# First-layer mixture of experts taken per batch half, its biases as bf16 rows, and the next attention begun on the first half

## The reference, cut to what matters

```python
# L0_ffn: x has L = 2 "positions" (the batches), so softmax over two keys
y1 = ln(x + mha(x), ln1_g, ln1_b)                 # 4 heads of 32
gates = softmax(y1 @ wg)                          # 8 experts, top one
keep = (rank of the token within its expert) < 128    # tokens counted in order
h = disp @ w1 + b1                                # no activation between
y = h @ w2 + b2
y2 = ln(y1 + where(keep, gate * y, 0), ln2_g, ln2_b)
x = ln(x + y2)
# L1_attn: 16 heads of 64 over 512 keys of the same batch
q, k, v = x @ w_q, x @ w_k, x @ w_v
x = ln(2 * x + softmax(q k^T / 8) v @ w_o)
```

## Time and profile before

| what | us |
|---|---|
| median of the runs | 761.89 |
| the profiled execution | 762.34 |
| its span, first to last instruction | 760.5 |
| mean granted clock of TensorE | 0.942 of full speed |
| PE busy / DVE / ACT / POOL | 686.6 / 455.1 / 278.2 / 238.8 |

### The profile page before, as it was taken

How to read it: one execution, slowest core, us unless ns; L and a number is a source line. 1 busy time by engine, 2 the same in 40 slices (tenths; PEclk the granted TensorE clock), 3 DMA queues, 4 the chain that set the end, 5 groups by cost and what they waited for, 6 DMA issues and landing times.

```text
span 760.5 us, 8997 instructions
## 1 busy us (share of the span) xinstructions
PE 686.6 (90%) x3300; PEld 343.1 (45%) x3300; DVE 455.1 (60%) x1181; ACT 278.2 (37%) x525; POOL 238.8 (31%) x161
## 2 busy tenths in 40 slices
PE   8746689999999999999999999989969999999996
PEld 5323487875553332222222222355422445656655
DVE  6997985653539656767667667445564554233334
ACT  7979863122010225444443444400224023121220
POOL 3895714110100204553644545524614000000001
PEclk9858979999789999999999999999979779999999
DMA  8100050110000000000000000004100000000000
GB/s 330 44 0 0 2 224 2 59 53 1 0 1 0 0 1 0 1 0 1 1 0 1 1 0 1 1 1 173 63 1 1 0 1 1 1 1 0 1 1 28
DMA packets 3682, 18.94 MB, mean 25 GB/s; under 512 B 917, under 2 KB 2198, under 8 KB 3126
## 3 DMA queue, kind: packets, MB, share of 16 engines
q1 hardware_dynamic: 3638, 18.36, 6.3%
HBM read 17.84 MB, written 0.52 MB: 24 GB/s over the span
## 4 chain that ended last, share of the span: by engine, by line
PE 66%; DVE 15%; POOL 10%; issue 5%; ACT 4%; POOLq 0%; DVEq 0%; ACTq 0%
PE PS L1984 11%; PE PS L1467 7%; PE PS L1998 6%; DVE SB L1621 5%; PE PS L1451 4%; PE PS L1422 4%; PE PS L243 3%; PE PS L1435 3%; DVE SB L1370 2%; PE PS L1483 2%; PE PS L1505 2%; PE PS L1550 2%; PE PS L1782 2%; PE PS L1793 1%; DVE SB L177 1%
## 5 line engine op out<-in xcount | busy, mean ns | idle before, releaser
L1604 POOL TENSOR_TENSOR SB<-SB 128x1024 f32<-128x1024 f32 x32 | 75.2, 2349 | 127.8 <-ACT SB L1574 127.7
L1621 DVE TENSOR_REDUCE SB<-PS 128x2 f32<-128x1024 f32 x64 | 78.4, 1226 | 52.7 <-PE PS L1435 52.6
L1574 ACT ACTIVATE SB<-PS 128x1024 f32<-128x1024 f32 x64 | 65.6, 1024 | 104.9 <-PE PS L1454 104.9
L223 POOL TENSOR_TENSOR SB<-SB 128x4 f32<-128x4 f32 (+1 forms) x18 | 17.8, 988 | 272.7 <-DVE SB L182 272.5
L1984 PE MATMUL PS<-SB 128*128 128x512 f32 x176 | 83.9, 618 | 0.0
L243 PE MATMUL PS<-SB 128*128 128x512 f32 (+1 forms) x158 | 74.1, 622 | 1.5 <-DVE SB L320 1.1
L1451 PE MATMUL PS<-SB 64*128 64x512 f32 x256 | 68.9, 616 | 0.0
L1467 PE MATMUL PS<-SB 128*64 128x512 f32 x256 | 67.8, 610 | 1.2 <-DVE SB L1658 1.2
L2064 DVE TENSOR_TENSOR SB<-SB,PS 128x512 f32<-128x512 f32 (+1 forms) x48 | 33.0, 688 | 54.0 <-PE PS L1984 50.0
L1654 DVE RECIPROCAL SB<-PS 128x512 f32<-128x512 f32 x16 | 53.7, 3358 | 17.6 <-PE PS L1483 17.6
L2022 ACT ACTIVATE SB<-PS 128x512 f32<-128x512 f32 (+1 forms) x48 | 28.6, 596 | 88.5 <-PE PS L1984 88.5
(11 more groups left out here) (369 smaller groups left out, 1144.3 us busy)
## 6 DMA issues: line engine op xcount, KB each, us to landing
SB<-exp SPq DMA_DIRECT2D x1, 4352.0 KB, 13.4
SB<-moe SPq DMA_DIRECT2D x1, 4096.0 KB, 12.1
SB<-dft SPq DMA_DIRECT2D x1, 2304.0 KB, 11.6
SB<-att SPq DMA_DIRECT2D x1, 2048.0 KB, 8.1
SB<-mix SPq DMA_DIRECT2D x1, 768.5 KB, 4.5
SB<-mix SPq DMA_DIRECT2D x1, 640.0 KB, 5.6
SB<-ssm SPq DMA_DIRECT2D x1, 602.0 KB, 6.7
SB<-lat SPq DMA_DIRECT2D x1, 585.0 KB
```

What stands on the lines that cost most here:

```text
L1574: act.activation(expd[i % 2][:, 1024 * u:1024 * u + 1024], bank(2 * (u % 2), 2), ACT.Exp).then_inc(sem("d_exp"), 1)
L1604: pool.tensor_tensor(half_sums[half], e[:, 0:1024], e[:, 1024:], ALU.add).then_inc(sem("d_half_sum"), 1)
L1621: dve.tensor_reduce(shift[i % 2][:, qt:qt + DK + 1:DK], two_heads(bank(4, 2)), AX_X, ALU.max, negate=True)\
```

## The change

1. `norm_gain` replaces, at the end of the block before and in stage c, the application of the norm followed by a product with the gain and a sum: (x - mean) * gain is taken while POOL computes the power, then * rstd + residual. The residual sums (`with_ob`, `with_n2b`) are made on POOL.
2. The projections of stage c are started on the first half; key and value differences are accumulated in PSUM with negated weights (`kv_minus`). The output bias matmuls (L1243) are gone. The bias merge goes to four column groups of the array. The weight merge is cut in pieces between other work.
3. POOL splits merged_bias in three bf16 rows, and lays them out beside each expert (`bias_rows`); PE adds them to each expert tile with a bf16 matmul. Transposes of the coefficients, their copy, the bias product and the full-width addition are gone. `y1` comes from a second transposition of `y1T`, copied by ACT.
4. The count before a token takes seven matmuls instead of a running count on DVE.
5. Experts are closed per half: norms of the first half stand between the scaled additions, and the query, key and value projections of stage d for the first half are issued before the second half is done. All value tiles are copied by ACT. The `stay_warm` calls in both stages are gone.

```diff
+    def norm_gain(dve, follow, src, gain, centred, plus, out, k):
+
+        norm_stats(dve, follow, src, k)
+        tiles = range(NT // 2 * k, NT // 2 * k + NT // 2)
+        for t in tiles:
+            ins = dve.scalar_tensor_tensor(centred[:, t, :], src[:, t, :], moments[:, 2 * t:2 * t + 1], gain, ALU.subtract,
+                                           ALU.mult)
+        follow(ins)
         norms[0] += 1
         dve.wait_ge(sem("norm_rstd"), norms[0])
         for t in tiles:
-            ins = dve.tensor_scalar(out[:, t, :], src[:, t, :], moments[:, 2 * t:2 * t + 1], rstd[:, t:t + 1],
-                                    ALU.subtract, ALU.mult)
-        return ins
+            ins = dve.scalar_tensor_tensor(out[:, t, :], centred[:, t, :], rstd[:, t:t + 1], plus[:, t, :], ALU.mult, ALU.add)
+        follow(ins)
...
+            pe.matmul(o, zeros_low, zeros_low, start=True, stop=False)
+            for e in range(E0):
+                for k in range(4):
+                    ins = pe.matmul(o[32 * k:32 * k + 8, :], mha["m_b1"][:, 64 * k + 8 * e:64 * k + 8 * e + 8],
+                                    moe["m_w2"][:, 128 * (4 * e + k):128 * (4 * e + k) + 128], start=False, stop=(e == E0 - 1),
+                                    tile_position=(0, 32 * k))
+            ins.then_inc(sem("c_merged"), 1)
+
...
+        half_turn(tiled(xs), "stage_half", 2, 0, 0)
+        merge_biases()
+        pe.wait_ge(sem("x_half_in"), 3)
+        pe.matmul(bank(7), wq, first, start=True, stop=True).then_inc(sem("c_qkv"), 1)
+        pe.matmul(bank(4), wk, first, start=True, stop=False)
+        pe.matmul(bank(5), wv, first, start=True, stop=False)
+        spread_biases()
+        merge(range(0, 2))
+        pe.wait_ge(sem("c_merged_in"), 3)
+        half_turn(tiled(xs), "stage_done", 2, 1, 1)
         pe.wait_ge(sem("turned_in"), 3)
+        pe.matmul(bank(4), kv_minus[:, 0:128], second, start=False, stop=True).then_inc(sem("c_qkv"), 1)
+        pe.matmul(bank(6), wq, second, start=True, stop=True).then_inc(sem("c_qkv"), 1)
+        pe.matmul(bank(5), kv_minus[:, 128:256], second, start=False, stop=True).then_inc(sem("c_qkv"), 1)
...
+        def count_before():
+
+            pe.wait_ge(sem("g_hot"), 2)
+            pe.matmul(bank(5)[:, 64:128], mha["earlier"], g_hot, start=True, stop=False)
+            for s in range(1, NT):
+                ins = pe.matmul(bank(5)[:, 64 + E0 * s:128], ones, g_hot[:, 0:E0 * (NT - s)], start=False, stop=(s == NT - 1))
+            ins.then_inc(sem("g_counted"), 1)
+
...
+        half_turn(tiled(xn), "c_half", 1, 0, 0)
+        half_turn(tiled(xn), "c_normed", 1, 1, 1)
+        logits(0)
+        rows_again(0)
+        logits(1)
+        pe.wait_ge(sem("c_merged_in"), 5)
+        expert(0)
+        rows_again(1)
+        count_before()
+        expert(1)
+        pe.wait_ge(sem("c_bias_row"), 1)
+        bias(0)
+        bias(1)
+        pe.wait_ge(sem("c_y1_in"), 2)
+        expert(2)
+        bias(2)
         pe.wait_ge(sem("g_coef"), 1)
+        expert(3)
+        bias(3)
+        for t in range(4, 7):
+            pe.wait_ge(sem("c_added"), 2 * E0 * (t // 2 - 1))
+            expert(t)
+            bias(t)
+        expert(7, (0,))
+        bias(7, (0,))
+
+        half_turn(tiled(xs), "stage_half", 3, 0, 4)
+        pe.wait_ge(sem("x_half_in"), 5)
+        pe.wait_ge(sem("att_in"), 16)
+        project(0, 0, 4)
+        pe.wait_ge(sem("c_added"), 6 * E0)
+        project(0, 1, 3)
+        expert(7, (1,))
+        bias(7, (1,))
...
+        pool.wait_ge(sem("c_merged_in"), 3)
+        follow(pool.tensor_copy(high_16, merged_bias))
+        follow(pool.tensor_tensor(rest_1, merged_bias, high_16, ALU.subtract))
+        follow(pool.tensor_copy(mid_16, rest_1))
+        follow(pool.tensor_tensor(rest_2, rest_1, mid_16, ALU.subtract))
+        follow(pool.tensor_copy(parts_16[0:32, :], high_16[0:32, :]))
+        follow(pool.tensor_copy(parts_16[32:64, :], mid_16[32:64, :]))
+        follow(pool.tensor_copy(parts_16[64:96, :], rest_2[64:96, :]))
+        pool.tensor_tensor(bias_rows.rearrange("p (e d) -> p e d", e=E0), parts_16[:, None, :].to_broadcast([P, E0, 128]),
+                           group_sum[:, 0:E0, None].to_broadcast([P, E0, 128]), ALU.mult).then_inc(sem("c_bias_row"), 1)
+        for k in range(2):
+            pool_rstd_half(pool, k)
+        for k in range(2):
+            half = slice(4 * k, 4 * k + 4)
+            pool.tensor_tensor(tiled(with_n2b)[:, half], tiled(xs)[:, half], four("n2_b"), ALU.add).then_inc(sem("c_kept"), 1)
...
+        def close(k):
+            dve.wait_ge(sem("c_added"), 4 * E0 * (k + 1))
+            dve.wait_ge(sem("c_kept"), k + 3)
+            norm_gain(dve, follow, tiled(moe_sum), rows["n2_g"], tiled(xn), tiled(with_n2b), tiled(xsum), k)
+            norm_stats(dve, follow, tiled(xsum), k)
+
+        combine(0, 0, E0)
+        combine(2, 0, E0)
+        close(0)
+        combine(4, 0, 2)
+        norm_apply(dve, tiled(xsum), tiled(xs), 0).then_inc(sem("stage_half"), 1)
+        combine(4, 2, E0)
+        combine(6, 0, E0)
+        close(1)
+        follow(dve.tensor_tensor(own_tile, ident[:, 0:4], ident[:, DK:DK + 4], ALU.add))
+        dve.wait_ge(sem("d_ones"), 3)
+        maximum(0, 0)
+        norm_apply(dve, tiled(xsum), tiled(xs), 1).then_inc(sem("stage_done"), 1)
 
 
...
+        values(0)
+        pe.wait_ge(sem("c_added"), NT * E0)
+        project(1, 0, 6)
+        pe.wait_ge(sem("d_qk_in"), 4)
+        values(1)
+        maxima(0, 0)
+        project(1, 1, 7)
+        values(2)
+        values(3)
+        pe.wait_ge(sem("stage_done"), 3)
+        pe.wait_ge(sem("d_qk_in"), 6)
+        for t in range(4):
+            ins = pe.transpose(bank(6)[:, 128 * t:128 * t + 128], tiled(xs)[:, 4 + t], ident)
+        ins.then_inc(sem("turned"), 1)
+        maxima(0, 1)
+        pe.wait_ge(sem("turned_in"), 5)
+        values(4)
+        maxima(0, 2)
+        values(5)
+        maxima(0, 3)
+        values(6)
         pe.wait_ge(sem("d_ones"), 3)
         shifts(0)
```

More of the change, by code:

```diff
@@ L1247, in c_pe @@
-        stay_warm(pe, 5, 5)
-        turn_pe(pe, tiled(xn), 0, (sem("c_normed"), 1), (sem("c_half"), 1))
-        stay_warm(pe, 1, 5)
-        pe.wait_ge(sem("turned_in"), 4)
-        for t in range(NT):
-            ins = pe.matmul(bank(5)[:, E0 * t:E0 * t + E0], y1T[:, 128 * t:128 * t + 128], mha["m_wg"], start=True, stop=True)
-        ins.then_inc(sem("g_logits"), 1)
-        stay_warm(pe, 4, 2)
-        pe.wait_ge(sem("g_hot"), 1)
-        pe.matmul(bank(6)[:, 0:NT * E0], mha["earlier"], g_hot, start=True, stop=False)
@@ L1259, in c_pe @@
-        pe.matmul(bank(6)[:, 0:NT * E0], ones, by_tile, start=False, stop=True).then_inc(sem("g_counted"), 1)
-        pe.wait_ge(sem("g_coef"), 1)
-        for t in range(NT):
-            ins = pe.transpose(PS[0:E0, 128 * t:128 * t + 128], g_coef[:, E0 * t:E0 * t + E0], ident)
-        ins.then_inc(sem("g_coef_turned"), 1)
-        stay_warm(pe, 1, 2)
-        pe.wait_ge(sem("g_coef_in"), 1)
-        for t in range(NT):
-            ins = pe.matmul(PS[:, 3072 + 128 * t:3072 + 128 * t + 128], coef_T[0:E0, 128 * t:128 * t + 128],
-                            merged_bias[0:E0, :], start=True, stop=True)
@@ L1269, in c_pe @@
[L1269 to L1280 removed]
+            pe.wait_ge(sem("c_qdk"), n + 1)
@@ new lines, in c_pe @@
+            pe.matmul(bank(n), mha["head_sum"], q_dk[:, 512 * n:512 * n + 512], start=True, stop=True).then_inc(sem("c_scores"), 1)
+        pe.wait_ge(sem("c_v_in"), 1)
+        pe.matmul(bank(4), wv, second, start=True, stop=True).then_inc(sem("c_qkv"), 1)
+        merge(range(2, 3))
+        for n in range(2):
+            pe.wait_ge(sem("c_attended"), n + 1)
+            for t in range(4 * n, 4 * n + 4):
+                ins = pe.matmul(PS[:, 3072 + 128 * t:3072 + 128 * t + 128], attended[:, 128 * t:128 * t + 128], mha["ow_T"],
+                                start=True, stop=True)
+            ins.then_inc(sem("c_out"), 1)
@@ new lines, in c_pe, with logits, rows_again @@
+        merge(range(3, E0))
+        def logits(h):
+            pe.wait_ge(sem(("x_half_in", "turned_in")[h]), 4)
+            for t in range(4 * h, 4 * h + 4):
+                ins = pe.matmul(bank(5)[:, E0 * t:E0 * t + E0], y1T[:, 128 * t:128 * t + 128], mha["m_wg"], start=True, stop=True)
+            if h:
+                ins.then_inc(sem("g_logits"), 1)
+        def rows_again(h):
+            for t in range(4):
+                ins = pe.transpose(bank(6 + h)[:, 128 * t:128 * t + 128], y1T[:, 512 * h + 128 * t:512 * h + 128 * t + 128], ident)
+            ins.then_inc(sem("c_y1"), 1)
@@ L1330, in c_dve @@
-        follow(dve.tensor_tensor(tiled(y1_bias), tiled(xs), every(rows["n2_b"]), ALU.add))
+            follow(dve.tensor_tensor(xsum[:, c], with_ob[:, c], bank(6 + k), ALU.add))
+            norm_stats(dve, follow, tiled(xsum), k)
+        for k in range(2):
```

(6 more changed lines are left out.)

375 lines of the change are left out of this document (193 added, 182 removed).

## The result

The changed kernel takes 729.07 us (median of four runs, 728.36 to 730.64) against 761.81 of the kernel before on the same chip: ratio 0.957, 95% interval 0.955 to 0.959. Forecast were 725.0 and a range of 719.5 to 734. The profiled execution took 728.36, with a span of 726.5.

A forecast was written before the change was run, and what follows sets the result against it. From 180 to 283 us the kernel was taken as a relay between engines, mostly TensorE. Savings of 5.6 + 11.6 + 12.1 - 7.0 + 4.9 + 13.2 = 40.4, less 3.5 for the clock, gave 725.0 us, range 719.5 to 734.

The forecast's parts named there:

- End of the block before: Up to stage c's second transposes: shorter norm and shorter TensorE queue move them from 180.1 to 174.55, saving 5.6 us.
- Turn to norm: Stage c's second transposes to the end of its first norm: 16.0 us against 27.5, saving 11.6.
- Norm to the first addition: End of stage c's first norm to the first scaled addition: 10.0 us against 22.1 at full clock, saving 12.1.
- The additions: The 64 scaled additions, with two norms of the first half among them: 23.6 us against 16.6, costing 7.0.
- Last addition to stage_done: Last scaled addition to stage_done: 8.0 us against 12.9, saving 4.9.
- To the first score: stage_done to the attention loop's first score: 10.8 us against 24.1, saving 13.2.
- Behind it: Everything from the first score to the end of the span keeps its instructions and its length.
- Rival 1: Clock stays low through routing, experts and additions (190 to 232): first score at 258.1, time 736.7 us; chance 0.12.
- Rival 2: Bias merge's column groups do not overlap: merge 7.2 us, second transposes 4.4 later, time 729.4; chance 0.06.
- Rival 3: POOL becomes the bound through slow broadcast operations: first power 20.5 us late, time 745.5; chance 0.03.
- Rival 4: Slower than before: without fillers, clock at 1.2 GHz from projections to loop, every PE leg doubles, 774.3 us; chance 0.02.
- Rival 5: Stage d's projections still wait for the second half; four value tiles, 6.9 us, come back: 731.9; chance 0.02.

The follow-up runs named there:

- serial_bias: Changed kernel with the bias merge in one column group instead of four, the same 64 records; 736.28 us, ratio 0.966 to the kernel before.
- sums_early: Changed kernel with GpSimd's two sums of xs and n2_b issued ahead of its first two powers; 724.06 us, ratio 0.953 to the kernel before.
- three_edits: Changed kernel with early GpSimd sums, four unread matmuls ahead of the first half's transposes at 221.8, one between the halves' transposes near 190; 722.32 us.
- warm_gap1: Changed kernel with two unread 128x512 matmuls in TensorE's idle between the two halves' transposes at 190 to 192.8; 725.71 us, ratio 0.951.
- before_cold: Kernel before, without the 36 unread matmuls (nine stay_warm calls) of the two stages; 769.37 us, ratio 1.009 to the kernel before.
- warm_gap2: Changed kernel with four unread 128x512 matmuls in TensorE's idle ahead of the first half's transposes at 221.8; 726.52 us, ratio 0.956.
- tile7_first: Changed kernel with the second half of expert tile 7 issued ahead of the key projection; 728.38 us, ratio 0.958 to the kernel before.
- gain_alone: Kernel before with only norm_gain added in the block before; 761.56 us, ratio 0.999 to the kernel before.

## Why the prediction was right, and where it was not

The sum was 36.9; the first score moved 33.7.

- *End of the block before*, 5.6: measured 5.5. But the margin was thin. I had TensorE ready at 173.3 and waiting for 1.3; it waited 0.20, so that `serial_bias` lost 5.0 of the 5.3 that its merge is longer. TensorE was ready at 174.4, not at 173.3. The bias merge took 1.93, where 1.6 was taken. The estimate from the Trainium skill ("TensorE: Matmul & The Clock Gate", section Measured speedup vs the span model), 3.0, goes by the ratio for three column tiles, and the 3.7 times of the four groups here is above that ratio. With 3.0 TensorE would have been ready at 174.7, behind 174.55, so "PE would still wait" was off by a little too.
- *Turn to norm*, forecast 16.0, measured 18.1. The step that failed: "POOL's two sums (2 x 1.1) and the bias rows are issued ahead of its powers" prices the sums of `with_ob` alone (they took 2.50). The two sums of `with_n2b`, which in the diff stand behind the first two powers, have no term in the prediction. They ran beside the application of the second half, and the price was VectorE's. Without the overlap the leg is 16.0 (in `sums_early`, 175.66 to 191.62). Worth 2.1.
- *Norm to the first addition*, forecast 10.0 plus 3.5 for one fall of the clock: 12.9, and 9.6 without a fall. Place and size were right (3.3 against 3.5), the cause only in part: I named transposes with idle between them, and the idle came mainly of the overlap above.
- *The additions*, forecast 23.6, measured 25.3, and 23.7 where the clock stays up. The step that failed is "A second, in the 4.4 us of idling, is hidden, since the query projection waits for the additions anyway". The fall began where I put it, but it outlasted the idling: the projections took 3.78 in place of 1.9, and expert tile 7's second half stands behind them. Worth 1.6.
- *Last addition to stage_done*, 8.0: 7.76. *To the first score*, 10.8: 10.95. *Behind it*, unchanged: 476.9 against 477.2.
- The two misses, 2.1 and 1.6, less 0.5 from legs a little shorter than taken, are the 3.2 us. At full clock and without the overlap the sum gave a first score at 242.9; `three_edits` has it at 242.4.
- Rival 1 (low clock through the experts) did not come: the clock was back at 201. The sentence from the Trainium skill beside it ("TensorE: Matmul & The Clock Gate", Part 4: PE-mode transpose), that a transposition is no work for the clock, fits the fall in the kernel after but does not foretell it: in `warm_gap1`, behind two unread matmuls, the same four transposes and sixteen 8-column records ran at 1.00. Rival 2 would have been dear, as `serial_bias` shows, more than the 4.4 I gave it. Rival 3: GpSimd's bias rows ended at 181.7 and its first power was wanted at 186.3. Rival 4 (slower): `before_cold` shows its mechanism at work in the kernel before, at a price of 7 us, not the 53. Rival 5: the value projections ran from 228.5, ahead of `stage_done`.
- Of its own signs of being right, the prediction met the turn at 174.6 and the unchanged loop and missed five: the norm's end (192.7 for 190.5), the first addition (205.6 for 200 to 204), the spread of the additions (25.3 for 23 to 24), `stage_done` (238.6 for 235) and the first score (249.6 for 245 to 248), all late by the two misses above. One sign of being wrong came, a wait of VectorE for TensorE of 1.79 us inside the additions; `warm_gap2` and `tile7_first` trace it to the clock and the order of the two projections. The time alone would not have told the forecast with its clock falls (up to 730.2) from rival 2 (729.4); the merge of 1.93 us does.
- What the runs leave open: two of the large savings, on the way to the norm and from there to the first addition (9.4 and 9.2 us), are measured as legs only. No run takes out the negated weights, the count in seven matmuls, the bf16 bias rows or the second transposition by themselves, so what each of them gave stands as the prediction argued it. And up to 2.4 of the 9.2 belong to the clock of that one profile before, if the execution of `gain_alone` is the measure.

## What to carry to other kernels

Price every operation that a change leaves on GpSimd twice: as time in its own queue, and as time taken from a VectorE `tensor_scalar` from SBUF to SBUF that it may run beside, the one form seen to lose time here; moving two sums ahead by nearly 8 us was worth 5. When a relay is shortened and its fillers go, look where TensorE waits ahead of work that it bounds itself, and put unread matmuls into just those waits: two were worth 3.3 us here, four others 1.5. Shortening a norm gains nothing while the engine that waits for it is still behind its own queue: shorten that queue first, then the norm.

## What the runs showed that I had not expected

- Two 128x512 sums of SBUF tensors on GpSimd nearly stop a row of 128x128 `tensor_scalar` on VectorE: 2.14 us lost in 2.50 of overlap, and nothing lost by 32 scaled additions that read PSUM.
- One such stall had an echo larger than itself: 2.1 us of VectorE's time became 2.1 of idle TensorE, and then 3.3 of low clock.
- Four column groups ran 64 records in 1.93 us where one group takes 7.21.
